# Two-layer graph kernel: column halves stored in another order by block, and second-layer masks read from the ring

## The chip, the cores and the metric

One core of a Trainium2 chip runs the kernel. The metric is the device time of one execution in microseconds. Three runs of the kernel before took 457.03, 455.23 and 456.34 us; their median is 456.34 us.

## The reference, cut to what matters

`x` is 4096 x 64, `adj` is 4096 x 4096 of zeros and ones (symmetric here, with ones on the diagonal, about one entry in 500 set). A first layer is graph attention over a second set of 4096 embeddings, a second layer is a sum over neighbours:

```python
h = jnp.maximum(_layernorm(x), 0.0)
Wh, We = h @ W, entity_embs @ W
scores = (Wh @ a1)[:, None] + (We @ a2)[None, :]
e = jnp.where(scores > 0, scores, ALPHA * scores)
e = jnp.where(adj > 0, e, NEG_BIG)
x = x + elu(softmax(e, axis=1) @ entity_embs + h)
h = jnp.maximum(_layernorm(x), 0.0)
x = x + (adj == 1) @ h + h
```

The second layer needs `h` of a row only after the first layer is done for that row, and all of `adj` a second time.

## The kernel before

**First layer.** The 4096 rows are taken in five blocks of 512, 512, 1024, 1024 and 1024 rows (`HALVES`), the 4096 columns in 32 tiles of 128. The loop runs over 160 steps n, 32 for each block: block 0 has steps 0 to 31, block 2 steps 64 to 95, block 3 steps 96 to 127, block 4 steps 128 to 159. In a step VectorE makes y from a tile of the masks and the scores (L788), ScalarE takes its exponential (L570), and TensorE multiplies it with the embeddings and adds to the block's accumulators (L1042). `yp` has four buffers (`YS`), so VectorE can be four steps ahead of TensorE. Each engine has one program, written out in order by the same loop; a step's extra work is placed by tables of step numbers.

**Masks.** `adj` lies in HBM transposed, as 64 chunks of 128 x 2048 int32 (1 MB each), which a GpSimd-issued DMA turns into bf16 in one of 23 buffers of `am`, the ring (`load`, L344 to 351). A buffer is free when y of its last step has been made. Blocks 2 to 4 have 16 chunks each, one for two steps. Before VectorE makes y it puts the row's shift into the chunk by an exclusive or over all of it (`put_shift`, L698 to 704), so from then on the chunk holds no plain zeros and ones. The shift of a block is found ahead of it: TensorE sums all its masks by column group (`biggest`, L897), VectorE reads the sums (`read_sums`, L667), TensorE turns them (`turn`, L909), VectorE takes the largest (`largest`) and works out the shift (`shifts`), TensorE spreads it to rows (`v_rows`, L917), ScalarE copies it to `vx` (L497), and VectorE does the lone rows (L714) and the first `put_shift`. For block 3 the last sums are at step 88 and `v_rows` at 94, for block 4 at 120 and 126.

**Between blocks.** After a block, ScalarE copies its row sums and numerators out (`sums_out`, L508 and L511) behind the exponential of the next block's second step, and TensorE's second pair of matmuls of the new block waits for that, since it writes into a bank just read. Then the block's rows go through inverse, elu, layer norm and a split into three bf16 parts `h3` (L720 to L758, by the steps in `FIN`): `h` of block 2 is complete at step 110, of block 3 at step 142, of block 4 in the tail.

**Second layer.** It is cut into 32 pieces (p, j): output rows of pair p (1024 rows), neighbours of column half j (512 columns). A piece can run once `h` of half j is there. It is four calls of `neighbours` (L950 to L972), each with six matmuls: three parts of `h` times two row halves, the masks as the moving operand. `ORDER` gives the sequence of the pieces and `PIECE_AT` the step at which each of the first 18 begins; each call stands behind the step's L1042 matmuls. The other 14 pieces follow after step 159. The masks of a piece are loaded a second time, as fp8, by GpSimd's queue (`load_edges`, L353 to 367): the first 16 into the four buffers of `edge`, the last 16 into ring buffers no longer needed. To pieces that hold a part of the diagonal GpSimd adds ones (`own`, L435 to L442). `VISITS` names the pieces after which the sum so far is copied out of bank 3 by ScalarE (`move_out`, L543, five steps after the piece begins) and added to `xs` by VectorE (`add_part`, at `PART_AT`).

The lines around the change, as the program has them before:

Of the kernel before, what the change touches and what calls it, by code (L numbers as in the profile page):

```python
# [5 lines left out]
P = 128  # L6
# [15 lines left out]
HALF = 512  # L22
# [19 lines left out]


ORDER = ((0, 0), (0, 1), (1, 0), (1, 1), (2, 0), (2, 1), (3, 0), (3, 1),
# [3 lines left out]
PIECE_AT = (78, 82, 87, 91, 96, 100, 105, 109, 114, 118, 123, 127, 131, 135, 140, 144, 149, 154)  # L48
PIECES = len(PIECE_AT)
VISITS = (1, 3, 5, 7)  # L50
OPENS = (0, 2, 4, 6, 8, 10, 12, 14)
PART_AT = (116, 120, 150)
EDGES = 4
RINGED = 16


def graph_layers(nc, adj_t, xt, ent, w_t, a_cols, eye, out, N, M, D):
# [12 lines left out]
    def width(b):  # L70
        return HALVES[b] * HALF

# [43 lines left out]
    with ctx:  # L116
        def sb(name, shape, dt):
            return ctx.enter_context(nc.sbuf_tensor(name, shape, dt))
# [9 lines left out]
        part = sb("part", [P, NP, HALF], F32)  # L128
# [65 lines left out]


        def ring_chunk(v):
            return NC - RING + v - RINGED

        def edges(v):
            if v < RINGED:  # L200
                flat = edge[:, v % EDGES]
            else:
                flat = am[:, ring_chunk(v) % RING].bitcast(FP8)
            return flat.rearrange("p (t i) -> p t i", t=4)

# [24 lines left out]
        edges_in = [sem(f"edges_in{v}") for v in range(len(ORDER))]  # L230
# [103 lines left out]
        def _(pool):  # L334
# [18 lines left out]
            def load_edges(v):  # L353
                p, j = ORDER[v]
                if v >= RINGED:
                    pool.wait_ge(y_made, step_past(ring_chunk(v)))
                elif v >= EDGES:
                    pool.wait_ge(piece_done, v - EDGES + 1)
# [5 lines left out]
                else:  # L364
                    q = chunk0[p + 1] + 2 * j
# [79 lines left out]
            def edges_at(v):  # L445
                if v >= RINGED:
                    return max(116 + 3 * (v - RINGED), step_past(ring_chunk(v)))
                return PIECE_AT[v - EDGES] + 5 if v >= EDGES else PIECE_AT[v] - 16

            q, v = 16, 0  # L450
            for n in range(STEPS_ALL):
# [4 lines left out]
                while v < len(ORDER) and edges_at(v) <= n:  # L456
                    load_edges(v)
                    v += 1
# [5 lines left out]
            for w in range(v, len(ORDER)):  # L464
                load_edges(w)
# [7 lines left out]
        def _(act):  # L473
# [92 lines left out]
            for n in range(STEPS_ALL):  # L566
# [3 lines left out]
                sc.activation(y, y, ACT.Exp, bias=tbias[:, jt:jt + 1]).then_inc(exp_done, 1)  # L570
# [34 lines left out]
        def _(dve):  # L605
# [171 lines left out]
            for n in range(STEPS_ALL):  # L777
# [10 lines left out]
                v.scalar_tensor_tensor(out=yp[:, n % YS, 0:W], in0=s8b[:, b % 2, 0:W], scalar=t8neg[:, jt:jt + 1],  # L788
# [38 lines left out]
            link(add_part(len(PART_AT)))  # L827
# [7 lines left out]
        def _(pe):  # L835
# [49 lines left out]
            def biggest(b, k):  # L885
# [7 lines left out]
                for i in range(m):  # L893
                    for g in range(4):
                        jt = 4 * k + g
                        at = jt % T * W + i * HALF
                        mm = t.matmul(pa[g * KC:(g + 1) * KC, i], gtab[:, jt],  # L897
# [52 lines left out]
            def neighbours(v, i):  # L950
                p, j = ORDER[v]
                jt = j * SUB + i
                if i == 0:
                    pe.wait_ge(edges_in[v], 32 if p == 0 else 16)
# [7 lines left out]
                    if v == 10:  # L962
                        pe.wait_ge(gmax_ready, NB)
                    if v == 14:
                        pe.wait_ge(num_sb, first[NB - 2] + 2)
                for k in range(3):
                    for s in range(2):
                        mm = t.matmul(gather(v)[s * D:(s + 1) * D, :], h3[:, jt, k * D:(k + 1) * D],  # L968
                                      edges(v)[:, i, s * HALF:(s + 1) * HALF],
# [45 lines left out]
            for n in range(STEPS_ALL):  # L1015
# [22 lines left out]
                for h in range(first[b], first[b + 1]):  # L1038
# [3 lines left out]
                    mm = t.matmul(acc(h)[0:D + 1, :], enta[:, jt], yp[:, n % YS, i * HALF:(i + 1) * HALF],  # L1042
# [65 lines left out]
```

## Time and profile before

| | |
|---|---|
| Median of three runs | 456.34 us |
| The profiled execution | 455.4 us |
| its span in the trace | 453.6 us |
| TensorE matmul busy | 414.5 us |
| VectorE busy | 317.7 us |
| ScalarE busy | 196.0 us |
| GpSimd busy | 126.9 us |
| Read from HBM | 136.63 MB |
| Mean granted TensorE clock | 0.969 |

The span is what the trace covers, from the first to the last instruction; the profiled execution's own time is 1.8 us more. A row of the timeline merges neighbouring instructions of one line: its start, its length, and in brackets how long the engine had been idle before it and who ended that. A matmul of 32-bit numbers is two instructions, so a step of a 1024-row block is four L1042 rows (x4). In the stretches, PEclk is the granted clock as a share of 2.4 GHz.

### The profile page before, as it was taken

The page shows a single profiled execution, that of the slowest core. Times are in us where ns is not written, and L with a number is a line of the kernel's source. Part 1 is how long each engine was busy: PE and PEld are TensorE (multiplying, and loading weights), DVE is VectorE, ACT ScalarE, POOL GpSimd, SP SyncE. Part 2 cuts the span into 40 slices and gives each one's busy share as a digit, 9 for nine tenths or more (in the row PEclk, how much of TensorE's full clock was granted, in tenths as well). Part 3 has the DMA queues.
Part 4 walks back from the last instruction along what each step waited for, and adds up shares of the span by engine and source line. Part 5 has one row for each costly group of instructions (what it writes and reads, how often), then busy time and mean ns, then how long its engine had stood idle before and what let it go on. Part 6 is the DMA issues. An engine that isn't in the chain of part 4 may idle for free. (4 is left out here: it accounts for less than half of the span.)

```text
span 453.6 us, 4680 instructions
## 1 busy us (share of the span) xinstructions
PE 414.5 (91%) x1786; PEld 143.1 (32%) x1791; DVE 317.7 (70%) x379; ACT 196.0 (43%) x250; POOL 126.9 (28%) x190
## 2 busy tenths in 40 slices
PE   2895997989878899999799999999699999999997
PEld 1562522223212232223122322232123222224564
DVE  3555779998899989659759576767958778723211
ACT  1310454665555656424644644424544544433200
POOL 7599200103022186111102320122042662000400
PEclk9879699999999999999989999999899999999999
DMA  8999999646459999799968998354539999999111
GB/s 270 214 212 215 214 214 171 107 84 102 81 92 149 154 142 161 100 144 159 137 108 85 117 148 124 40 49 45 46 30 103 108 107 106 105 107 108 18 44 50
DMA packets 25382, 54.09 MB, mean 119 GB/s; under 512 B 1872, under 2 KB 10128, under 8 KB 25104
## 3 DMA queue, kind: packets, MB, share of 16 engines
q0 software_dynamic: 24192, 50.34, 79.2%
q1 hardware_dynamic: 1008, 3.42, 2.0%
q8 instruction: 14, 0.23, 0.2%
q10 hardware_dynamic: 160, 0.03, 0.0%
q14 instruction: 8, 0.07, 0.0%
HBM read 136.63 MB, written 1.05 MB: 304 GB/s over the span
## 5 line engine op out<-in xcount | busy, mean ns | idle before, releaser
L1042 PE MATMUL pb<-yp,enta 128*65 128x512 f32 x512 | 247.4, 609 | 18.0 <-ACT yp L570 11.7
L570 ACT ACTIVATE yp<-yp,tbias 128x1024 f32<-128x1024 f32 (+1 forms) x160 | 153.9, 979 | 126.8 <-DVE yp L788 125.8
L788 DVE SCALAR_TENSOR_TENSOR yp<-s8b,t8neg,am 128x1024 f32<-128x1024 f32 (+1 forms) x160 | 168.4, 1079 | 31.4 <-PE pb L1042 29.4
L1042 PEld LDWEIGHTS pb<-yp,enta 128*65 128x65 f32 x512 | 61.9, 138 | 154.3 <-issue 104.3
L703 DVE TENSOR_TENSOR am<-am,vx 128x2048 uint16<-128x2048 uint16 x64 | 79.0, 1234 | 0.7 <-ACT vx L497 0.7
L351 POOL DMA_DIRECT2D am<-adj_t x64 | 35.4, 557 | 130.3 <-DVE yp L788 130.3
L968 PE MATMUL pb<-edge,h 128*64 128x512 fp8e4 x288 | 40.9, 392 | 0.0
L366 POOL DMA_DIRECT2D edge<-adj_t x12 | 8.7, 725 | 79.2 <-PE pb L968 54.1
L968 PEld LDWEIGHTS pb<-edge,h 128*64 128x64 bf16 x288 | 12.3, 109 | 44.4 <-issue 39.6
L968 PE MATMUL pb<-am,h 128*64 128x512 fp8e4 x192 | 22.7, 381 | 0.0
L968 PE MATMUL pa<-am,h 128*64 128x512 fp8e4 x192 | 21.7, 380 | 0.0
L897 PE MATMUL pa<-am,gtab 128*32 128x512 bf16 x256 | 20.7, 392 | 0.0
L431 POOL TENSOR_SCALAR rstd<-rstd 128x8 f32<-128x8 f32 x5 | 2.1, 418 | 58.1 <-ACT rstd L529 58.0
L968 PEld LDWEIGHTS pb<-am,h 128*64 128x64 bf16 x192 | 11.4, 110 | 13.6 <-issue 6.8
L968 PEld LDWEIGHTS pa<-am,h 128*64 128x64 bf16 x192 | 11.8, 110 | 10.2 <-issue 2.5
L442 POOL TENSOR_TENSOR edge<-edge,eyeb 128x128 fp8e4<-128x128 fp8e4 x16 | 15.0, 964 | 0.1
L667 DVE TENSOR_SCALAR gmax<-pa,wk 128x1024 f32<-128x1024 int32 (+1 forms) x5 | 5.4, 1071 | 13.2 <-PE pa L897 13.2
L968 PE MATMUL pa<-edge,h 128*64 128x512 fp8e4 x96 | 14.1, 402 | 0.0
L745 DVE TENSOR_TENSOR rs<-pa,rstd 128x512 f32<-128x512 f32 (+1 forms) x5 | 2.9, 585 | 15.2 <-POOL rstd L432 15.2
L729 DVE TENSOR_TENSOR ta<-num,pa 128x512 f32<-128x512 f32 x5 | 3.4, 686 | 12.1 <-PE pa L933 12.1
L897 PEld LDWEIGHTS pa<-am,gtab 128*32 128x32 bf16 x256 | 4.2, 94 | 23.9 <-issue 23.8
L489 ACT COPY s8b<-pa 128x512 f32<-128x512 f32 x8 | 4.7, 583 | 16.1 <-PE pa L875 16.1
(144 smaller groups left out, 292.2 us busy)
## 6 DMA issues: line engine op xcount, KB each, us to landing
am<-adj_t POOLq DMA_DIRECT2D x76, 512.0 KB, 9.8
edge<-adj_t POOLq DMA_DIRECT2D x12, 512.0 KB, 8.1
edge<-adj_t POOLq DMA_DIRECT2D x8, 256.0 KB, 7.6
am<-adj_t POOLq DMA_DIRECT2D x8, 256.0 KB, 23.9
enta<-ent SPq DMA_DIRECT2D x1, 1040.0 KB, 5.1
xs<-xt SPq DMA_DIRECT2D x1, 1024.0 KB, 8.3
out<-yp SPq DMA_DIRECT2D x4, 256.0 KB, 2.0
mats<-eye SPq DMA_DIRECT2D x1, 256.0 KB, 5.4
```

What stands on the lines that cost most here:

```text
L351: pool.dma_start(am[:, q % RING], adj_t[q]).then_inc(landed[q % RING], 16)
L366: pool.dma_start(edges(v).rearrange("p (c t) i -> p c (t i)", c=2), adj_t[q:q + 2].rearrange("c p n -> p c n")).then_inc(edges_in[v], 16)
L442: g.tensor_tensor(e, e, eyeb[:], ALU.add, saturate=False).then_inc(own_ready, 1)
L489: sc.copy(s8b[:, b % 2, i * HALF:(i + 1) * HALF], bank_s(b, i)).then_inc(s8_ready, 1)
L570: sc.activation(y, y, ACT.Exp, bias=tbias[:, jt:jt + 1]).then_inc(exp_done, 1)
L667: link(v.tensor_scalar(gmax[:, 0:W], sums, wk[:], None, ALU.min))
L703: v.tensor_tensor(at, at, vx[:, b % 2, 0:width(b)].bitcast(U16).unsqueeze(1).to_broadcast([P, tiles(b), width(b)]), ALU.bitwise_xor).then_ ...
L729: link(v.tensor_tensor(ta[:], num[:], turned, ALU.mult))
L788: v.scalar_tensor_tensor(out=yp[:, n % YS, 0:W], in0=s8b[:, b % 2, 0:W], scalar=t8neg[:, jt:jt + 1], in1=am[:, (chunk0[b] + c) % RING, jt ...
L897: mm = t.matmul(pa[g * KC:(g + 1) * KC, i], gtab[:, jt], am[:, (chunk0[b] + jt // T) % RING, at:at + HALF], start=(k == 0), stop=(k == NQ ...
L968: mm = t.matmul(gather(v)[s * D:(s + 1) * D, :], h3[:, jt, k * D:(k + 1) * D], edges(v)[:, i, s * HALF:(s + 1) * HALF], start=(v in OPENS ...
L1042: mm = t.matmul(acc(h)[0:D + 1, :], enta[:, jt], yp[:, n % YS, i * HALF:(i + 1) * HALF], start=(jt == 0), stop=(jt == NT - 1))
```

## The change

The chunks of blocks 2 to 4 hold their column halves in another order (`COLUMNS`): block 2 ends with halves 0 and 1, block 3 with 0 to 3, block 4 has 6, 7 and then 0 to 5. Everything that goes by column tile (`t8neg`, `tbias`, `gtab`, `enta`) is indexed through `tile_at`. So chunks whose halves have their `h` early now lie in the ring, loaded and not yet shifted, when their piece can run. 12 pieces (`DIRECT`) read their masks there, as bf16, and are not loaded a second time; `put_shift` of each of their chunks waits for the piece. The order of the pieces, the steps at which they begin, the steps of the loads and the banks of the sums are changed to fit: three partial sums are moved out instead of four, and pair 3 keeps its bank.

```diff
+COLUMNS = ((0, 1, 2, 3, 4, 5, 6, 7), (0, 1, 2, 3, 4, 5, 6, 7), (2, 3, 4, 5, 6, 7, 0, 1),
+           (4, 5, 6, 7, 0, 1, 2, 3), (6, 7, 0, 1, 2, 3, 4, 5))
...
-ORDER = ((0, 0), (0, 1), (1, 0), (1, 1), (2, 0), (2, 1), (3, 0), (3, 1),
...
+ORDER = ((1, 0), (1, 1), (0, 0), (0, 1), (2, 0), (2, 1), (2, 2), (2, 3), (3, 0), (3, 1), (3, 2), (3, 3),
+         (0, 2), (0, 3), (3, 4), (3, 5), (1, 2), (1, 3),
...
-PIECE_AT = (78, 82, 87, 91, 96, 100, 105, 109, 114, 118, 123, 127, 131, 135, 140, 144, 149, 154)
+PIECE_AT = (70, 80, 85, 89, 96, 100, 111, 115, 120, 124, 128, 132, 136, 140, 144, 148, 152, 156)
-VISITS = (1, 3, 5, 7)
-OPENS = (0, 2, 4, 6, 8, 10, 12, 14)
-PART_AT = (116, 120, 150)
+DIRECT = (0, 1, 4, 5, 6, 7, 8, 9, 10, 11, 14, 15)
+LOADED = tuple(v for v in range(len(ORDER)) if v not in DIRECT)
+VISITS = (1, 3, 7)
+OPENS = (0, 2, 4, 8, 12, 16, 22)
+PART_AT = (118, 122, 154)
-RINGED = 16
+RINGED = 6
+LOAD_AT = (48, 54, 62, 70, 94, 98)
...
+        def masks(v, i, s):
+            if v in DIRECT:
+                at = i % 2 * 2 * HALF + s * HALF
+                return am[:, chunks_of(*ORDER[v])[i // 2] % RING, at:at + HALF]
+            return edges(v)[:, i, s * HALF:(s + 1) * HALF]
...
-            return pb[:, 3] if v <= VISITS[-1] else (pb[:, 3], pa[:, 0], pa[:, 1], pb[:, 2])[p]
+            return pb[:, 3] if v <= VISITS[-1] else (pa[:, 0], pa[:, 1], pb[:, 2], pb[:, 3])[p]
...
             def put_shift(b, c):
                 q = chunk0[b] + c
                 if c == 0:
                     dve.wait_ge(vx_ready, first[b + 1])
+                for w in DIRECT:
+                    if q in chunks_of(*ORDER[w]):
+                        dve.wait_ge(piece_done, w + 1)
...
-            link(add_part(len(PART_AT)))
...
                 if i == 0:
-                    pe.wait_ge(edges_in[v], 32 if p == 0 else 16)
+                    if v in DIRECT:
+                        for q in chunks_of(p, j):
+                            pe.wait_ge(landed[q % RING], 16 * (q // RING + 1))
+                    else:
+                        pe.wait_ge(edges_in[v], 32 if p == 0 else 16)
```

Where the instructions stand is shown at three places. In the changed program the lines are numbered anew: L897 is L927, L917 is L947, L968 (the six matmuls of a `neighbours` call) is L1002, L1042 is L1076, L543 is L569, L570 is L597, L497 is L523, L508 and L511 are L534 and L537.

TensorE, from the mask sums of step 92 over `v_rows` (step 94) to the first matmuls of step 96, before:

```order
L897 MATMUL pa<-am,gtab 32x512 x8
L1042 MATMUL pb<-yp,enta 65x512 x2
L968 MATMUL pb<-edge,h 64x512 x6
L1042 MATMUL pb<-yp,enta 65x512 x2
L968 MATMUL pb<-edge,h 64x512 x6
L917 MATMUL pa<-vd,onesb 128x512 x2
L1042 MATMUL pb<-yp,enta 65x512 x2
L968 MATMUL pb<-edge,h 64x512 x6
L1042 MATMUL pb<-yp,enta 65x512 x2
L897 MATMUL pa<-am,gtab 32x512 x8
L1042 MATMUL pb<-yp,enta 65x512 x2
```

and now:

```order
L927 MATMUL pa<-am,gtab 32x512 x8
L1076 MATMUL pb<-yp,enta 65x512 x2
L1002 MATMUL pb<-edge,h 64x512 x6
L1076 MATMUL pb<-yp,enta 65x512 x2
L947 MATMUL pa<-vd,onesb 128x512 x2
L1076 MATMUL pb<-yp,enta 65x512 x4
L927 MATMUL pa<-am,gtab 32x512 x8
L1076 MATMUL pb<-yp,enta 65x512 x2
```

The calls of `neighbours` behind steps 93 and 94 are gone from here. Block 2 has 16 of them before and now: before at steps 78 to 85 and 87 to 94, now at 70 to 73, 80 to 83 and 85 to 92.

ScalarE, the exponentials and copies from step 80 to 97 (vx is the shift, part the partial sum, rows and num the old block's sums), before:

```order
L570 ACTIVATE yp<-yp,tbias 128x1024 x7
L543 COPY part<-pb 128x512
L570 ACTIVATE yp<-yp,tbias 128x1024 x8
L497 CAST vx<-pa 128x512 x2
L570 ACTIVATE yp<-yp,tbias 128x1024
L543 COPY part<-pb 128x512
L570 ACTIVATE yp<-yp,tbias 128x1024
L508 COPY rows<-pb 1x512 x2
L511 COPY num<-pb 64x512 x2
```

and now:

```order
L597 ACTIVATE yp<-yp,tbias 128x1024 x5
L569 COPY part<-pb 128x512
L597 ACTIVATE yp<-yp,tbias 128x1024 x9
L569 COPY part<-pb 128x512
L597 ACTIVATE yp<-yp,tbias 128x1024
L523 CAST vx<-pa 128x512 x2
L597 ACTIVATE yp<-yp,tbias 128x1024 x2
L534 COPY rows<-pb 1x512 x2
L537 COPY num<-pb 64x512 x2
```

The second copy of a partial sum has moved from behind the exponential of step 96 to behind that of step 94, ahead of the two copies to vx.

TensorE, from step 104 on, before:

```order
L897 MATMUL pa<-am,gtab 32x512 x8
L943 MATMUL pa<-mats,tm 128x2 x4
L946 MATMUL pa<-mats,ta 128x128 x4
L1042 MATMUL pb<-yp,enta 65x512 x4
L968 MATMUL pb<-edge,h 64x512 x6
L1042 MATMUL pb<-yp,enta 65x512 x2
L968 MATMUL pb<-edge,h 64x512 x6
L1042 MATMUL pb<-yp,enta 65x512 x2
L968 MATMUL pb<-edge,h 64x512 x6
L897 MATMUL pa<-am,gtab 32x512 x8
L1042 MATMUL pb<-yp,enta 65x512 x2
```

and now:

```order
L927 MATMUL pa<-am,gtab 32x512 x8
L973 MATMUL pa<-mats,tm 128x2 x4
L976 MATMUL pa<-mats,ta 128x128 x4
L1076 MATMUL pb<-yp,enta 65x512 x8
L927 MATMUL pa<-am,gtab 32x512 x8
L1076 MATMUL pb<-yp,enta 65x512 x2
L905 MATMUL pa<-h,w 128x512
L1076 MATMUL pb<-yp,enta 65x512 x4
L905 MATMUL pa<-h,w 128x512
L1076 MATMUL pb<-yp,enta 65x512 x2
L1002 MATMUL pb<-am,h 64x512 x6
```

Steps 105 to 110 have lost their `neighbours` calls (step 104 had none before either); the next one stands behind step 111.

## Rows read from the trace of the kernel before

**Rows 1.** Page of the profile: part 1, and what HBM moved

```profile
PE 414.5 (91%) x1786; PEld 143.1 (32%) x1791; DVE 317.7 (70%) x379; ACT 196.0 (43%) x250; POOL 126.9 (28%) x190
...
HBM read 136.63 MB, written 1.05 MB: 304 GB/s over the span
```

**Rows 2.** Waits: engine line waited for: us in total, times, longest us

```profile
DVE yp L788 <- PE pb L1042: 29.4, 28, 2.0
...
PE pb L1042 <- ACT num L511: 6.1, 2, 3.1
```

**Rows 3.** Stretches: length, busy us per engine, PEclk, DMA share, GB/s

```profile
160.00:180.00 20.00, 20.00 (x71) 6.08 (x72) 18.36 (x18) 12.30 (x15) 16.01 (x15) 1.00 1.01 162
...
220.00:240.00 20.00, 16.74 (x65) 4.25 (x68) 14.74 (x16) 9.68 (x12) 1.78 (x3) 0.91 0.71 102
```

**Rows 4.** TensorE timeline, steps 69 and 78: start, us, what, [idle before <- whom]

```profile
151.60 3.65 PE L1042 MATMUL pb<-yp,enta 128*65 128x512 f32 x8 [1.20 <-ACT yp L570]
...
174.42 0.84 PE L968 MATMUL pb<-edge,h 128*64 128x512 fp8e4 x6
```

**Rows 5.** TensorE timeline, steps 85 to 87, one slice and none

```profile
193.11 1.93 PE L1042 MATMUL pb<-yp,enta 128*65 128x512 f32 x4
194.98 0.84 PE L968 MATMUL pb<-edge,h 128*64 128x512 fp8e4 x6
195.74 3.65 PE L1042 MATMUL pb<-yp,enta 128*65 128x512 f32 x8
199.32 0.84 PE L968 MATMUL pb<-edge,h 128*64 128x512 fp8e4 x6
```

**Rows 6.** TensorE timeline, steps 88 to 96, the first border

```profile
200.09 0.61 PE L897 MATMUL pa<-am,gtab 128*32 128x512 bf16 x8
...
218.07 0.38 PE L917 MATMUL pa<-vd,onesb 128*128 128x512 bf16 x1 [0.16 <-issue]
...
223.54 1.07 PE L1042 MATMUL pb<-yp,enta 128*65 128x512 f32 x2 [0.20 <-ACT yp L570]
227.67 1.97 PE L1042 MATMUL pb<-yp,enta 128*65 128x512 f32 x2 [3.06 <-ACT num L511]
```

**Rows 7.** ScalarE timeline at the same border

```profile
215.38 2.35 ACT L570 ACTIVATE yp<-yp,tbias 128x1024 f32<-128x1024 f32 x2 [2.65 <-DVE yp L788]
218.27 1.07 ACT L497 CAST vx<-pa 128x512 bf16<-128x512 f32 x2 [0.54 <-remote]
...
225.84 1.18 ACT L508 COPY rows<-pb 1x512 f32<-1x512 f32 x2
```

**Rows 8.** VectorE timeline at the same border

```profile
200.76 1.28 DVE L667 TENSOR_SCALAR gmax<-pa,wk 128x1024 f32<-128x1024 int32 x1 [4.39 <-PE pa L897]
...
219.38 0.42 DVE L714 TENSOR_SCALAR rows<-vx 3x1024 bf16<-3x1024 bf16 x1 [2.83 <-ACT vx L497]
```

**Rows 9.** TensorE timeline, steps 120 to 128, the second border

```profile
298.30 0.61 PE L897 MATMUL pa<-am,gtab 128*32 128x512 bf16 x8
...
314.82 0.38 PE L917 MATMUL pa<-vd,onesb 128*128 128x512 bf16 x1 [0.16 <-issue]
...
321.46 1.07 PE L1042 MATMUL pb<-yp,enta 128*65 128x512 f32 x2 [0.97 <-ACT yp L570]
325.60 1.18 PE L1042 MATMUL pb<-yp,enta 128*65 128x512 f32 x2 [3.06 <-ACT num L511]
```

**Rows 10.** ScalarE timeline at the second border

```profile
316.21 1.05 ACT L497 CAST vx<-pa 128x512 bf16<-128x512 f32 x2
```

**Rows 11.** VectorE timeline, y of step 108

```profile
257.57 1.28 DVE L788 SCALAR_TENSOR_TENSOR yp<-s8b,t8neg,am 128x1024 f32<-128x1024 f32 x1
```

**Rows 12.** TensorE timeline, step 108

```profile
264.45 1.93 PE L1042 MATMUL pb<-yp,enta 128*65 128x512 f32 x4
```

**Rows 13.** GpSimd timeline, own() of the first piece

```profile
165.26 4.16 POOL L442 TENSOR_TENSOR edge<-edge,eyeb 128x128 fp8e4<-128x128 fp8e4 x4
```

**Rows 14.** VectorE timeline beside it

```profile
164.37 1.53 DVE L788 SCALAR_TENSOR_TENSOR yp<-s8b,t8neg,am 128x1024 f32<-128x1024 f32 x1
```

More of the change, by code:

```diff
@@ L71, in width, with tile_at, place @@
         return HALVES[b] * HALF
+    def tile_at(b, jt):
+        return COLUMNS[b][jt // SUB] * SUB + jt % SUB
+    def place(b, j):
+        return COLUMNS[b].index(j)
     def tiles(b):
@@ L127, in graph_layers @@
         edge = sb("edge", [P, EDGES, 2 * CHUNK], FP8)
-        part = sb("part", [P, NP, HALF], F32)
+        part = sb("part", [P, len(VISITS), HALF], F32)
         yp = sb("yp", [P, YS, 2 * HALF], F32)
@@ L192, in graph_layers, with chunks_of, ring_chunk @@
         arep = am[0:D, 22].bitcast(F32)[:, 0:P]
-        def ring_chunk(v):
-            return NC - RING + v - RINGED
+        def chunks_of(p, j):
+            q = chunk0[p + 1] + 2 * place(p + 1, j)
+            return q, q + 1
+        def ring_chunk(u):
+            return NC - RING + u - RINGED
         def edges(v):
-            if v < RINGED:
-                flat = edge[:, v % EDGES]
+            u = LOADED.index(v)
+            if u < RINGED:
+                flat = edge[:, u % EDGES]
             else:
-                flat = am[:, ring_chunk(v) % RING].bitcast(FP8)
+                flat = am[:, ring_chunk(u) % RING].bitcast(FP8)
             return flat.rearrange("p (t i) -> p t i", t=4)
+        def masks(v, i, s):
[3 more added lines that the diff above has]
+            return edges(v)[:, i, s * HALF:(s + 1) * HALF]
         pa = ps("pa", [P, 4, HALF])
@@ L229, in graph_layers @@
         landed = [sem(f"landed{k}") for k in range(RING)]
-        edges_in = [sem(f"edges_in{v}") for v in range(len(ORDER))]
+        edges_in = {v: sem(f"edges_in{v}") for v in LOADED}
         out_done = sem("out_done")
@@ L351, in load, with load_edges @@
                 pool.dma_start(am[:, q % RING], adj_t[q]).then_inc(landed[q % RING], 16)
-            def load_edges(v):
+            def load_edges(u):
+                v = LOADED[u]
                 p, j = ORDER[v]
[L355 to L358, printed above, removed]
+                if u >= RINGED:
+                    pool.wait_ge(y_made, step_past(ring_chunk(u)))
+                elif u >= EDGES:
+                    pool.wait_ge(piece_done, LOADED[u - EDGES] + 1)
                 if p == 0:
@@ L455, in _ @@
                     q += 1
-                while v < len(ORDER) and edges_at(v) <= n:
-                    load_edges(v)
-                    v += 1
+                while u < len(LOADED) and edges_at(u) <= n:
+                    load_edges(u)
+                    u += 1
                 if b >= 1 and jt == FIN[b - 1]["vs"] + 1:
@@ L1076 @@
     r = 0
-    for m in HALVES:
+    for m, order in zip(HALVES, COLUMNS):
         t = 4 // m
-        a = np.asarray(adj)[r:r + m * HALF].reshape(m * HALF, NT // t, t, P).transpose(1, 3, 2, 0)
+        a = np.asarray(adj)[r:r + m * HALF].reshape(m * HALF, M // HALF, HALF)[:, list(order)]
+        a = a.reshape(m * HALF, NT // t, t, P).transpose(1, 3, 2, 0)
         parts.append(a.reshape(NT // t, P, CHUNK))
```

28 lines of the change are left out of this document (13 added, 15 removed), and 3 rows, old and new, of the table ORDER.

## The prediction

> **What bounds the kernel now.** I read part 1 of the page first: TensorE is busy 414.5 of 453.6 us, VectorE 317.7 [rows 1]. Then the stretches: from 160 to 180 us TensorE is busy 20.00 of 20 [rows 3], and the stretches behind it look the same except around two places. Then the waits: VectorE waits for TensorE 28 times [rows 2], so it runs ahead by the four buffers of yp and is held back by TensorE. The TensorE timeline says where that begins: its last plain idle time before a piece is 1.20 us ahead of step 69 [rows 4], and from there to the tail it stands still only at the borders of the last blocks. So from step 70 the time is TensorE's work plus the idle time at the borders. I write "slice" for the six matmuls of `neighbours()` in one step, and "pv" for the step's main matmuls.
>
> A step with a slice takes 195.74 - 193.11 = 2.63 us, two without take 199.32 - 195.74 = 3.58, or 1.79 each [rows 5]. A slice is worth **0.84 us**, wherever it stands.
>
> The two idle places are steps 96 and 128. The first matmul pair of the block waits 0.20 or 0.97 us for the exponential, the second 3.06 us for ScalarE to copy the old accumulator out [rows 6, 9]; both together are the two waits of 6.1 us [rows 2]. What ends there is a chain which starts at the last mask sums (L897, steps 88 and 120): VectorE's read of the sums at 200.76 [rows 8], the turn, the largest, the shift, `v_rows` on TensorE (218.07), the copies to vx on ScalarE (218.27) [rows 7], the lone rows (219.38) [rows 8], two y, and ScalarE's row copies from 225.84 [rows 7]. The pair of matmuls after the wait takes 1.97 us against 1.07 for the pair ahead of it [rows 6], with the granted clock at a mean of 0.91 in that stretch [rows 3].
>
> **The change, part by part.**
>
> *Slices moved.* The table still holds 72 slices in the loop and 56 behind it, so TensorE's sum is unchanged: 0. Four of them now stand at steps 70 to 73. TensorE had no idle time there to be filled (it lies ahead of step 69, [rows 4]), so they gain nothing.
>
> *First border.* Up to step 87 nine slices ran before, eleven will: the last mask sums come 2 x 0.84 = 1.7 us later. From there to the end of the wait the chain is 227.67 - 200.09 = 27.6 us [rows 6]. Inside it TensorE had seven slices to do, now five. The chain passes `v_rows` in TensorE's order, which is now one slice earlier, and ScalarE had waited 0.54 us for it [rows 7]. But the copy of a finished piece (L543), which stood behind the exponential of step 96, is moved between those of 94 and 95, just ahead of the vx copies, and takes about half the 1.18 us of two row copies [rows 7]. It uses up the 0.54. So the chain stays at 27.6 us with two slices less inside: **+1.7 us** of idle time (0.20 and 3.06 become about 2 and 3.1).
>
> *Steps 104 to 110* hold no slice now. VectorE finishes y of step 108 at 257.57 + 1.28 = 258.9, its exponential (half of the 2.35 us of two, [rows 7]) ends at 260.0, and TensorE comes to it at 264.45 [rows 11, 12]: 4.4 us of lead. The slices of 105 to 107 go, 2.5 us; 1.9 are left. After that both engines run at nearly one pace. I take 0.
>
> *Second border.* The chain from the mask sums at 298.30 to 325.60 takes 27.3 us [rows 9]. `v_rows` at 314.82 could be 0.84 later without delaying the vx copies of 316.21 [rows 9, 10], so the chain holds its length. Inside it are now eight slices instead of seven (step 122 was empty), and the eighth fits into the 0.97 us: **-0.8 us**.
>
> *Masks read from the ring as bf16.* No row shows such a slice. The nearest is L897, which streams bf16 columns of the same tile: eight matmuls in two packs of four last 0.61 us [rows 6], 0.305 a pack, against 0.84 / 3 = 0.28 a pair in a slice [rows 5]. The 12 pieces have 12 x 4 x 3 = 144 pairs, so between 0 and 144 x 0.025 = 3.6 us; a pack holds twice the matmuls of a pair, and I take 0.
>
> *Waits.* Each of the 12 pieces waits for two chunks instead of one load. The first slice of a piece, with its waits, starts in the row of 199.32 right when the pv ends [rows 5]: 0. VectorE's `put_shift` waits for the piece at steps 118, 122, 150 and 154. At 118 it already needs the pv of step 114 and now its slice too, 0.84 later. At 150 it needs the slice of 147 instead of the pv of 146: 0.84 + 1.79 + 0.84 = 3.5 us, and TensorE then has three steps of 2.63 in hand, 7.9 us, against some 1.3 us each for the shift, y and the exponential. Hidden. If TensorE's lead work were gone, each hold would cost its 3.5 us.
>
> *Loads and GpSimd.* 12 issues on its queue go. The others are issued behind the chunk loads of their step. No TensorE wait for a chunk is in the rows of the waits after the start: 0. The `own()` additions, 4.16 us a piece, ran beside a y that took 1.53 instead of 1.28 us [rows 13, 14, 11]; they move to steps 83 and 87, where VectorE waits anyway. Two such stretches of some 5 us, a fifth longer, are at most 2 us of VectorE time. TensorE was not idle there, so 0. The Trainium skill, "SBUF — State Buffer", section "Who interferes with whom", says that VectorE and GpSimd share a port pair which one of them takes whole; by that the 2 us are real, and the sum would be 2 us better only if VectorE set the pace at steps 76 to 83.
>
> *One partial sum less*: a copy of 0.6 us and an addition, the last of them behind `lasts`, while TensorE works: 0.
>
> Sum: 1.7 - 0.8 = **+0.9 us**. The profiled execution took 455.4 us, the median of the three runs is 456.34, 0.9 above it. So 456.3 in the first measure and **457.2** as a median.
>
> **Rivals.**
>
> *The empty steps starve TensorE (slower, 0.16).* It decides if y of step 108 comes more than 1.9 us later, relative to TensorE, than in the rows above. The chain of the standard deviation goes over ScalarE and GpSimd just there, and the first border starts it from a longer wait. For it: 1.9 us is the smallest lead of the loop. Against it: nothing in that chain is lengthened. The price is up to the three slices that no longer cover it, 2.5 us: 459.7.
>
> *The slow clock lasts longer behind the first border (slower, 0.05).* The pair there lost 0.9 us [rows 6]; a longer idle stretch ahead of it may cost as much again, and half of that in the next slice: 457.2 + 1.4 = 458.6.
>
> *The first border costs nothing (0.13).* If ScalarE finishes the extra copy while it waits anyway and VectorE was the longer branch, only the second border's gain is left or both cancel: 455.5 to 456.3.
>
> *Transfers were the bound after all (faster, 0.08).* The queues are full from 160 to 180 us (share 1.01, [rows 3]), and 12 loads of 2.1 MB, 25 of the 136.6 MB read [rows 1], go away. If one border wait hung on a late chunk, it would go with its slow pair: -3.06 - 0.9 = -4.0, 452.3. Against it: TensorE is busy 20.00 of 20 in that same stretch. The Trainium skill, the same page, section "A bandwidth-pool intuition that's wrong (but worth ruling out)", calls HBM almost always the end-to-end bottleneck; this trace does not agree after the start, where 304 GB/s [rows 1] go beside a full TensorE.
>
> *The change doesn't do what it says (0.02).* The loads could be issued all the same; the order of GpSimd's queue shows 20 pieces loaded, not 32, so hardly.
>
> **How the numbers follow.** The forecast has 0.56. About 0.5%, 2.3 us, is what a measurement of this kernel can tell from no change. Faster by more: the transfers, 0.08, and 0.02 of scatter (the three runs lie 1.8 us apart). Slower by more needs above 458.6: most of the empty steps (0.14), half of the clock (0.03) and 0.03 for the bf16 bound: 0.20. The rest, 0.70, is the same. The range goes from 0.9 us of scatter below the case 455.5, 454.6, to the bounds of the empty steps and of bf16 (457.2 + 2.5 = 459.7 and 457.2 + 3.6 = 460.8), so 460.8.
>
> **What would show it.** HBM read near 111 MB. L897 of step 88 near 201.8 us. Ahead of the first pair of step 96 about 2 us of idle time, ahead of the second about 3.1, with `v_rows` near 218.9. At step 128 next to nothing ahead of the first pair. No idle time from step 104 to 111. Slices from am that last 0.84 us like those from edge. Wrong would be: an idle TensorE anywhere between steps 70 and 95, or 104 and 120; a slice from the ring clearly above 0.84 us; VectorE waiting at L733 long enough to empty yp; or borders without idle time.

## The result, and the profile after

The changed kernel takes 457.92 us in the median of 8 runs (457.18 to 458.98), the kernel before 455.69 us in 8 runs (455.09 to 457.03), the three of the first section among them. The medians are 2.2 us apart; the ratio on record is 1.0039, 95% interval 1.0024 to 1.0053, which makes it 1.8 us slower. Both are under the 0.5% (2.3 us) that I had put as the bound. The forecast was 457.2 us, 0.9 us slower. Of the difference 0.3 us lies outside the span: the profiled execution took 457.4 us with a span of 455.3, 2.1 us apart where the kernel before had 1.8.

The page of the changed kernel, parts 1, 3 and 5:

```profile
PE 415.3 (91%) x1791; PEld 141.8 (31%) x1791; DVE 316.4 (69%) x378; ACT 194.8 (43%) x249; POOL 115.8 (25%) x178
...
HBM read 111.46 MB, written 1.05 MB: 247 GB/s over the span
...
L733 DVE TENSOR_TENSOR am<-am,vx 128x2048 uint16<-128x2048 uint16 x64 | 78.9, 1233 | 4.8 <-PE pb L1002 4.1
...
L1002 PE MATMUL pb<-am,h 128*64 128x512 bf16 (+1 forms) x432 | 57.2, 390 | 0.0
...
L1002 PE MATMUL pa<-edge,h 128*64 128x512 fp8e4 x96 | 13.4, 387 | 0.0
```

TensorE is as busy as before (415.3 to 414.5 us, [rows 1]); 25.2 MB less are read. A matmul on bf16 masks from the ring lasts 390 ns (the group holds the fp8 ones of bank pb too), one on fp8 masks from `edge` 387. VectorE stood still twice ahead of a `put_shift` (L733), 4.1 us in all.

The TensorE timeline of the changed kernel around the first border; it answers to [rows 4, 6] (L927 is L897, L947 is L917, L1076 is L1042, L1002 is L968):

```profile
151.40 3.65 PE L1076 MATMUL pb<-yp,enta 128*65 128x512 f32 x8 [1.20 <-ACT yp L597]
...
201.72 0.61 PE L927 MATMUL pa<-am,gtab 128*32 128x512 bf16 x8
...
218.61 0.59 PE L947 MATMUL pa<-vd,onesb 128*128 128x512 bf16 x2
...
224.83 1.07 PE L1076 MATMUL pb<-yp,enta 128*65 128x512 f32 x2 [1.65 <-ACT yp L597]
228.96 1.97 PE L1076 MATMUL pb<-yp,enta 128*65 128x512 f32 x2 [3.06 <-ACT num L537]
230.86 1.30 PE L1002 MATMUL pb<-am,h 128*64 128x512 bf16 x6
232.09 1.93 PE L1076 MATMUL pb<-yp,enta 128*65 128x512 f32 x4
```

Step 69 begins at 151.40 instead of 151.60, so 0.2 us are to be added in a comparison. The last mask sums are at 201.72 against 200.09: counted from step 69 1.8 us later, two slices and 0.15 us. The wait ends at 228.96, 27.24 us after them, where it was 27.58. Ahead of the first pair TensorE now stands still for 1.65 us. The second border, answering to [rows 9]:

```profile
294.53 0.61 PE L927 MATMUL pa<-am,gtab 128*32 128x512 bf16 x8
...
317.94 1.07 PE L1076 MATMUL pb<-yp,enta 128*65 128x512 f32 x2 [0.49 <-ACT yp L597]
322.08 1.97 PE L1076 MATMUL pb<-yp,enta 128*65 128x512 f32 x2 [3.06 <-ACT num L537]
323.98 1.49 PE L1002 MATMUL pb<-am,h 128*64 128x512 bf16 x6
325.40 2.91 PE L1076 MATMUL pb<-yp,enta 128*65 128x512 f32 x4
328.24 0.84 PE L1002 MATMUL pb<-am,h 128*64 128x512 bf16 x6
```

Two rows of the kernel before that the comparison below needs, the main matmuls of step 97 and the slice of step 129:

```profile
230.96 1.93 PE L1042 MATMUL pb<-yp,enta 128*65 128x512 f32 x4
...
330.83 0.84 PE L968 MATMUL pa<-edge,h 128*64 128x512 fp8e4 x6
```

At the second border the chain takes 322.08 - 294.53 = 27.55 us against 27.30, the first pair waits 0.49 us against 0.97, and the pair behind the wait takes 1.97 us where it took 1.18. Steps 104 to 111 and step 108, answering to [rows 11, 12]:

```profile
255.48 7.03 PE L1076 MATMUL pb<-yp,enta 128*65 128x512 f32 x16
...
262.99 1.93 PE L1076 MATMUL pb<-yp,enta 128*65 128x512 f32 x4
```

Four steps without a slice follow each other in 7.03 us, and no idle time stands ahead of any of these rows. The two spans differ by 1.7 us. Cut at the rows shown, they add up as follows:

| stretch of TensorE's timeline | before, us | now, us | difference, us |
|---|---|---|---|
| start to step 69 | 151.60 | 151.40 | -0.20 |
| step 69 to the end of the first wait | 76.07 | 77.56 | +1.49 |
| from there to the main matmuls of step 97 | 3.29 | 3.13 | -0.16 |
| from there to the end of the second wait | 94.64 | 89.99 | -4.65, with five slices fewer (4.20): -0.45 |
| from there to the slice of step 129 | 5.23 | 6.16 | +0.93 |
| from there to the end of the span | 122.77 | 127.06 | +4.29, with five slices more (4.20): +0.09 |

So the first border costs 1.49 us: the sums 1.83 later, less 0.34 for a shorter chain. The second gives back 0.45: the idle time ahead of its first pair falls from 0.97 to 0.49. Together that is 1.04 us. The slow rows behind the two waits give -0.16 and +0.93, start and end -0.20 and +0.09.

### The profile page after: what moved, and what is told of

Same layout as the page of the kernel before. It is cut to its first block and busy times, and to the rows that moved or that the text cites. A ratio compares the mean times of both kernels' runs of the same rounds, so it can differ in the third digit from the quotient of the medians.

```text
span 455.3 us, 4672 instructions
## 1 busy us (share of the span) xinstructions
PE 415.3 (91%) x1791; PEld 141.8 (31%) x1791; DVE 316.4 (69%) x378; ACT 194.8 (43%) x249; POOL 115.8 (25%) x178
## 5 line engine op out<-in xcount | busy, mean ns | idle before, releaser
L1076 PE MATMUL pb<-yp,enta 128*65 128x512 f32 x512 | 250.0, 613 | 18.9 <-ACT yp L597 12.7
L597 ACT ACTIVATE yp<-yp,tbias 128x1024 f32<-128x1024 f32 (+1 forms) x160 | 153.5, 977 | 129.1 <-DVE yp L819 128.0
L1076 PEld LDWEIGHTS pb<-yp,enta 128*65 128x65 f32 x512 | 61.9, 138 | 154.3 <-issue 106.5
L733 DVE TENSOR_TENSOR am<-am,vx 128x2048 uint16<-128x2048 uint16 x64 | 78.9, 1233 | 4.8 <-PE pb L1002 4.1
L380 POOL DMA_DIRECT2D am<-adj_t x64 | 35.4, 559 | 172.8 <-DVE yp L819 172.8
L1002 PE MATMUL pb<-am,h 128*64 128x512 bf16 (+1 forms) x432 | 57.2, 390 | 0.0
L1002 PEld LDWEIGHTS pb<-am,h 128*64 128x64 bf16 x432 | 21.9, 110 | 50.6 <-issue 39.8
L1002 PE MATMUL pa<-am,h 128*64 128x512 fp8e4 x192 | 21.6, 380 | 0.0
L927 PE MATMUL pa<-am,gtab 128*32 128x512 bf16 x256 | 20.9, 395 | 0.0
L396 POOL DMA_DIRECT2D am<-adj_t x10 | 7.1, 713 | 49.1 <-DVE yp L819 43.4
L472 POOL TENSOR_TENSOR edge<-edge,eyeb 128x128 fp8e4<-128x128 fp8e4 x16 | 16.0, 1026 | 0.1
L1002 PEld LDWEIGHTS pa<-am,h 128*64 128x64 bf16 x192 | 11.8, 110 | 9.8 <-issue 2.0
L1002 PE MATMUL pa<-edge,h 128*64 128x512 fp8e4 x96 | 13.4, 387 | 0.0
L927 PEld LDWEIGHTS pa<-am,gtab 128*32 128x32 bf16 x256 | 4.2, 94 | 25.5 <-issue 25.4
L542 ACT ACTIVATE tm<-ta 128x512 f32<-128x512 f32 x5 | 3.1, 628 | 19.6 <-DVE ta L760 19.6
L750 DVE STREAM_TRANSPOSE gmax<-rows 64x512 f32<-64x512 f32 x5 | 3.5, 708 | 10.7 <-ACT rows L534 10.4
```

The costliest lines, as they stand in the source:

```text
L380: pool.dma_start(am[:, q % RING], adj_t[q]).then_inc(landed[q % RING], 16)
L396: pool.dma_start(edges(v).rearrange("p (c t) i -> p c (t i)", c=2), adj_t[q:q + 2].rearrange("c p n -> p c n")).then_inc(edges_in[v], 16)
L472: g.tensor_tensor(e, e, eyeb[:], ALU.add, saturate=False).then_inc(own_ready, 1)
L597: sc.activation(y, y, ACT.Exp, bias=tbias[:, at:at + 1]).then_inc(exp_done, 1)
L733: v.tensor_tensor(at, at, vx[:, b % 2, 0:width(b)].bitcast(U16).unsqueeze(1).to_broadcast([P, tiles(b), width(b)]), ALU.bitwise_xor).then_ ...
L750: link(v.transpose(turn32, inv))
```

## Experiments

Twelve experiments on three chips, all against the kernel before on the same chip.

**Is it the slices inside the first chain?** Two kernels move pieces 1 to 3. In e1 seven slices stand between the sums of step 88 and the border, as before the change:

```diff
-PIECE_AT = (70, 80, 85, 89, 96, ...)
+PIECE_AT = (70, 82, 87, 91, 96, ...)
```

In e5 there are three:

```diff
-PIECE_AT = (70, 80, 85, 89, 96, ...)
+PIECE_AT = (70, 79, 83, 87, 96, ...)
```

> The changed kernel with pieces 1 to 3 begun at steps 82, 87 and 91 as before instead of 80, 85 and 89, so that seven slices stand again between the last mask sums of step 88 and the border of step 96, and the copy of the partial sum is behind step 96 again. My theory (the slices missing inside that fixed chain cost 0.84 us each): the idle time ahead of the first pair of step 96 falls from 1.65 to near 0.2 us and the whole is 1.3 us faster than the changed kernel, span near 454.0, ratio to the kernel before about 1.001. Rival (the changed kernel's loss sits elsewhere, in the slow clock or in the reads from the ring): span stays at 455.3.

> The same place the other way: pieces 1 to 3 begin at steps 79, 83 and 87, so that only three slices stand between the mask sums of step 88 and the border. My theory: two slices more are taken out of the chain's shadow, 2 x 0.84 = 1.7 us more idle time ahead of the first pair of step 96 (near 3.3 us), span near 456.9. Rival (the border's idle time does not depend on the slices): 455.3 as in the changed kernel.

Measured: e1 456.21 us (12 runs), ratio 0.9992 (0.9979 to 1.0006); e5 459.38 us (6 runs), ratio 1.0063 (1.0043 to 1.0083); between them, on the same chip, the changed kernel with added loads (e4, below) 457.64. That kernel has 0.3 us less outside its span than the other two, so the spans are compared, in runs of the same mean clock, 0.966: 454.25 us for e1 (8 runs), 455.70 for e4 (10 runs, and 455.70 for the changed kernel itself in 7), 457.16 for e5 (5 runs). So 1.45 us back and 1.46 more, for two slices each way. The idle rows of e5 at the border:

```profile
221.30 3.65 PE L1076 MATMUL pb<-yp,enta 128*65 128x512 f32 x8 [0.69 <-ACT yp L597]
...
227.59 1.07 PE L1076 MATMUL pb<-yp,enta 128*65 128x512 f32 x2 [2.10 <-ACT yp L597]
231.73 1.97 PE L1076 MATMUL pb<-yp,enta 128*65 128x512 f32 x2 [3.06 <-ACT num L537]
```

0.69 + 2.10 us of idle time stand ahead of the first pair instead of 1.65, and the 3.06 of the second pair is unchanged. From step 69 (152.81 us here) the second pair's wait ends after 78.92 us instead of 77.56, 1.36 more and not the 1.7 expected: the copy of the partial sum has left the chain in e5, which is 0.32 us shorter for it (26.92). In e1 the first pair waits 0.20 us, as before the change:

```profile
224.03 1.07 PE L1076 MATMUL pb<-yp,enta 128*65 128x512 f32 x2 [0.20 <-ACT yp L597]
228.16 1.07 PE L1076 MATMUL pb<-yp,enta 128*65 128x512 f32 x2 [3.06 <-ACT num L537]
```

The slices inside the chain are shown to be the cause at this border, at 0.73 us each by the runs. e1's chain is again 27.58 us long. e1 is level with the kernel before.

**The second chain.** The additions of partial sums are taken out of it:

```diff
-PART_AT = (118, 122, 154)
+PART_AT = (114, 118, 154)
```

> The changed kernel with the two first additions of partial sums on VectorE at steps 114 and 118 instead of 118 and 122, so that none lies inside the chain from the mask sums of step 120 to the border of step 128. My theory: the addition of 0.68 us at 299.99 us lengthened that chain; without it the second pair of step 128 starts 0.6 us earlier, idle ahead of the first pair falls from 0.49 to near 0, span near 454.7. Rival (VectorE has slack there, as I had costed it): no change, 455.3.

Measured: 457.46 us (12 runs), ratio 1.0022 (1.0007 to 1.0037), 0.2 us below the kernel with added loads on the same chip. By spans at the mean clock 0.966 it is 455.34 us (10 runs) against 455.70 (10 runs): 0.4 us of the 0.5 that the chain became shorter, and hardly clear of the scatter (454.5 to 456.4 in e2's ten runs). The profiled execution is the slowest of the twelve (458.51 us). In it the chain is shorter, and the time is lost again behind the borders:

```profile
295.80 0.61 PE L927 MATMUL pa<-am,gtab 128*32 128x512 bf16 x8
...
318.70 1.07 PE L1076 MATMUL pb<-yp,enta 128*65 128x512 f32 x2
322.84 1.97 PE L1076 MATMUL pb<-yp,enta 128*65 128x512 f32 x2 [3.07 <-ACT num L537]
324.74 1.49 PE L1002 MATMUL pb<-am,h 128*64 128x512 bf16 x6
326.16 3.25 PE L1076 MATMUL pb<-yp,enta 128*65 128x512 f32 x4
```

From the sums to the second pair 27.04 us instead of 27.55, and no idle time ahead of the first pair. But the matmuls of step 129 take 3.25 us instead of 2.91, and the rows behind the first border 0.17 us more than in the changed kernel: more of the work ran at the low clock. From step 69 to the end this execution takes 456.4 - 152.5 = 303.9 us, like the changed kernel's. That the shorter chain is lost on average is not shown: between the theory (0.6) and the rival (0), the runs lean to the theory.

**Transfers.** 12 loads come back, to a buffer of their own, at steps 66 to 123:

```diff
+            def load_again(k):
+                q = 36 + 2 * k
+                if k >= 1:
+                    pool.wait_ge(dup_in, 16 * k)
+                pool.dma_start(dup[:].rearrange("p (c n) -> p c n", c=2),
+                               adj_t[q:q + 2].rearrange("c p n -> p c n")).then_inc(dup_in, 16)
```

> The changed kernel with 12 loads of 2 MB read from HBM added on the same queue, to a buffer that nobody reads, at steps 66 to 123, so that about as much is read as before. My theory (transfers set the pace nowhere after the start): no change beyond 0.3 us, 455.3, with HBM read back near 136.6 MB. Rival (fewer transfers give time back which something else eats): 2 us or more slower than the changed kernel, 457.3 and up, with waits of TensorE or VectorE for a landed chunk.

Measured: 457.64 us (12 runs), ratio 1.0028 (1.0013 to 1.0043); its profiled span is that of the changed kernel, 455.3 us, and so is the median of its spans, 455.8. Outside the span it has 1.8 us again, like the kernel before, where the changed kernel has 2.1: those 0.3 us come and go with the twelve loads. How is not shown.

```profile
HBM read 136.63 MB, written 1.05 MB: 302 GB/s over the span
```

The 25.2 MB are back and cost nothing in the span. From step 66 on, transfers set the pace nowhere; the start was not tested.

**The clock behind the borders.** 12 matmuls which compute nothing stand where TensorE waits 3.06 us, in the changed kernel (e7, again as e11), in the kernel before (e9) and in e1 (e10):

```diff
+                    if jt == 0 and h >= 3 and i == 1:
+                        pe.wait_ge(vx_ready, first[b + 1])
+                        for k in range(KEEP):
+                            t.matmul(bank_s(b, k % 2), onesb[:], vd[:, 0:SUB].rearrange("p c k -> p (c k)"),
+                                     start=True, stop=True)
                     if jt == 0 and h >= 3:
                         pe.wait_ge(num_sb, h - 2)
```

> The changed kernel with 12 matmuls of 128x512 bf16 added on TensorE between the first and the second pair of steps 96 and 128, into a bank that nobody reads. They take no time from anything else (3.06 us of waiting stand there, they need about 2.7 us) and compute nothing. My theory: the granted clock then stays up behind both borders, the pairs and slices there take 1.07 and 0.84 us instead of 1.97 and 1.30 to 1.49, which gives back about 1.5 us at the first border and 2.6 at the second, 4 us in all, span near 451.3; the waits for ScalarE end where they ended. Rival (the slow rows behind the border are not the clock but the restart of the pipe): no change, 455.3.

Measured: 454.97 us (5 runs), ratio 0.9955 (0.9942 to 0.9968). Useless work makes the changed kernel 3 us faster. Two stretches of 12 us, one over each border, in the table of stretches of the changed kernel (columns as in [rows 3]):

```profile
224.00:236.00 12.00, 8.11 (x23) 2.04 (x24) 9.54 (x10) 7.68 (x9) 1.79 (x3) 0.86 0.85 119
318.00:330.00 12.00, 8.94 (x23) 2.21 (x24) 8.65 (x9) 6.90 (x8) 2.17 (x3) 0.72 1.06 85
```

The same stretches of e7:

```profile
224.00:236.00 12.00, 9.88 (x44) 3.13 (x44) 11.00 (x11) 8.05 (x9) 1.79 (x3) 1.00 0.83 123
318.00:330.00 12.00, 11.47 (x44) 3.55 (x44) 8.77 (x9) 6.91 (x9) 2.17 (x3) 1.00 1.04 85
```

And e7's TensorE timeline at the second border:

```profile
318.97 2.75 PE L1078 MATMUL pa<-vd,onesb 128*128 128x512 bf16 x12
322.19 1.07 PE L1081 MATMUL pb<-yp,enta 128*65 128x512 f32 x2 [0.47 <-ACT num L538]
323.20 0.84 PE L1003 MATMUL pb<-am,h 128*64 128x512 bf16 x6
```

The granted clock is 1.00 (2.4 GHz) where it had a mean of 0.86 and 0.72, that is, part of the stretch at 1.2 GHz. The pair behind the wait takes 1.07 us, not 1.97, and still begins at 322.19: the wait for ScalarE ends as before. So behind both borders the slow rows are the clock. In the changed kernel it fell while TensorE stood still: taken microsecond by microsecond at the second border, the granted clock is 1.00 up to 320, 0.79 to 321, 0.50 up to 327, 0.79 to 328 and 1.00 again, with the wait over at 322.08. In the kernel before it fell at the second border only after TensorE had begun again, between 326 and 327 us with the wait over at 325.60, and was back between 329 and 330; so its pair there took 1.18 us and only the slice and the matmuls behind it were slow.

I expected 4 us. From step 69, where the start is left out, to the end of the span it is 452.9 - 152.9 = 300.0 us instead of 455.3 - 151.4 = 303.9, the 3.9 us expected; the start took 1.5 us of them back in this execution. Over all runs the gain in the span is 3.0 us (a mean of 452.9 in e7 and in e11, 455.9 and 456.0 in the two batches of the changed kernel). The length of the start varies from 151.0 to 152.9 us in the profiles of the changed kernel and its variants, though none of their edits but e4's first load stands in it; why is open.

> The kernel before with the 12 idle matmuls in both waits, so that no border lowers the clock. My theory: the runs of the kernel before lie between 455.3 and 457.8 us by how much of the work behind the borders meets the low clock (their mean clock goes from 0.969 to 0.962), and with the clock held the borders' idle time alone is left: 0.75 us less than the changed kernel with the same matmuls, so span near 452.0 and a time near 453.9, and less scatter. Rival (the changed kernel's loss is a matter of the clock only): the same 452.9 and 455.0 as the changed kernel with them.

> The changed kernel with the 12 idle matmuls once more, beside the kernel before with them on the same chip. Theory: 455.0 us again, 0.8 to 1.1 us above the kernel before with them (0.75 for the borders, up to 0.3 outside the span). Rival (clock only): no difference between the two.

> The changed kernel with the idle matmuls and with seven slices inside the first chain. Theory: the first border's 1.3 us come back, free of the clock: 1.3 us below the changed kernel with the idle matmuls, near 453.7, and 0.3 to 0.6 below the kernel before with them in span, since the second border has its eighth slice. Rival: part of the 2.1 us between the changed kernel and the one with seven slices was the clock, and here it is under 0.8.

Measured on one chip: e9 454.21 us (9 runs, ratio 0.9946, 0.9927 to 0.9965), e11 454.89 us (12 runs, 0.9963, 0.9947 to 0.9978), e10 453.49 us (6 runs, 0.9938, 0.9916 to 0.9960). From step 69 to the end of the span, where the start is left out, e9 takes 452.1 - 153.2 = 298.9 us, e11 452.9 - 152.9 = 300.0 and e10 451.0 - 152.5 = 298.5. With the clock held, the change costs 1.1 us of span, and giving the first chain its seven slices takes 1.5 us off. Both are what the rows say: 1.49 - 0.45 + 0.09 = 1.13 by the table above, and 1.48 from step 69 to the end of the first wait (77.56 us in e11, 76.08 in e9 and e10). The 0.75 and 1.3 of the theories left out the 0.15 us ahead of the first chain and took 0.59 for the second border. The mean clock is 0.977 in all runs of e11, but 0.973 to 0.977 in e9 and e10, though in their profiles it is 1.00 over both borders: the clock of an execution varies in other places too. In the start of these profiles, between 20 and 60 us, it lies between 0.66 and 0.84.

> The changed kernel again, as it is, beside the others and the kernel before on one chip. Theory: its runs scatter with the mean clock as those of the kernel before do, 0.966 to 0.963 with 457.5 to 459, and its distance to the kernel before comes out between 0.7 and 2.5 us by the clocks that the two happen to draw. Rival (the longer low clock at its second border is its own): its mean clock never reaches the 0.969 of the kernel before, on any chip.

Measured: 457.89 us (12 runs), ratio 1.0036 (1.0021 to 1.0052). Its profile has the slow rows the other way round:

```profile
224.00:236.00 12.00, 7.88 (x21) 1.77 (x21) 9.77 (x10) 7.92 (x9) 1.79 (x3) 0.72 0.83 117
318.00:330.00 12.00, 8.45 (x28) 2.05 (x28) 9.93 (x10) 8.05 (x9) 2.17 (x3) 0.86 1.18 94
```

Now the mean is 0.72 over the first border and 0.86 over the second, in the same program. Put in order by the mean clock of the whole execution, the runs give (of the kernel before those beside the experiments, of the changed kernel those of the result and e12):

| mean granted clock | kernel before: runs, mean us | changed kernel: runs, mean us |
|---|---|---|
| 0.969 | 15, 455.3 | none |
| 0.965 | 18, 456.2 | none |
| 0.966 | 15, 457.1 | 16, 457.8 |
| 0.962 or 0.963 | 16, 457.8 | 4, 459.0 |

The kernel before lies anywhere between 455 and 458 us by how much of its work meets the low clock, and the execution profiled of it was one of the luckiest. Over all these runs the mean clock of the two kernels is the same, 0.9654, and their mean spans are 454.8 and 456.0 us: 1.2 apart, near the 1.1 that the borders give without the clock. So the 0.93 us behind the second border is a draw of the two executions that were profiled. What differs is the spread: the changed kernel and its variants with the longer idle time at the first border (e2, e4, e5) never had 0.969 or 0.965 in 50 runs, where 33 of 64 of the kernel before had, and e1, with the old idle time there, had 0.970 in 4 of 12. That speaks for the idle time as what keeps them from those cases; how, no run shows.

**A version that beats both.** If TensorE waits there, the slices that come next can run there. The four of steps 96 to 99 and of 128 to 131 are put between the two pairs, in the changed kernel (e3), in the kernel before (e6, there seven, those of 96 to 99 and of 128 to 130), and with the changes of e1 and e2 on top (e8):

```diff
+FILL = {96: ((4, 0), (4, 1), (4, 2), (4, 3)), 128: ((10, 0), (10, 1), (10, 2), (10, 3))}
+MOVED = sum(FILL.values(), ())
...
+                    if i == 1 and n in FILL:
+                        for k in FILL[n]:
+                            neighbours(*k)
                     if jt == 0 and h >= 3:
                         pe.wait_ge(num_sb, h - 2)
...
-                    if at <= n < at + SUB:
+                    if at <= n < at + SUB and (v, n - at) not in MOVED:
```

> The changed kernel with the four slices of steps 96 to 99 and the four of 128 to 131 placed between the first and the second pair of steps 96 and 128, where TensorE waits 3.06 us. My theory: eight slices leave the rest of the loop, six to eight times 0.77 to 0.84 us are gained, about 6 us, and the clock stays up as with added matmuls, 4 us: span near 446, if VectorE keeps up in steps 97 to 103 and 129 to 135. Rival (VectorE becomes the bound behind the border, since it starts the block late and has the inverses and the weighting there): only the clock's 4 us are gained, near 451.

> The same in the kernel before: the four slices of steps 96 to 99 and those of 128 to 130 stand inside the two waits. My theory: the same gain as in the changed kernel less one slice, so the kernel before with it stays 1 to 2 us ahead of the changed kernel with it, span near 445 to 446. Rival (reading from the ring pays once TensorE is no longer held): the changed kernel with filled waits is the faster.

> The changed kernel with filled waits, the old steps of pieces 1 to 3 (seven slices inside the first chain) and the partial sums added four steps earlier. My theory: another 1.3 us for the first border and 0.5 us for the second on top of the filled waits, near 444.5 and the fastest of all. Rival (with the waits filled the chain on VectorE and ScalarE sets the borders): within 0.5 us of the kernel with filled waits alone.

Measured on one chip: e3 446.85 us (5 runs), ratio 0.9777 (0.9764 to 0.9791); e6 446.89 us (4 runs), 0.9775 (0.9758 to 0.9791); **e8 444.78 us** (4 runs), 0.9735 (0.9717 to 0.9753). e8 around its first border:

```profile
222.93 1.07 PE L1081 MATMUL pb<-yp,enta 128*65 128x512 f32 x2 [0.20 <-ACT yp L599]
223.93 2.78 PE L1004 MATMUL pb<-am,h 128*64 128x512 bf16 x24
227.06 4.51 PE L1081 MATMUL pb<-yp,enta 128*65 128x512 f32 x10 [0.35 <-ACT num L539]
```

24 matmuls stand where nothing stood, 0.35 us of waiting are left, and the four steps' slices are gone from behind the border: five pairs (two and a half steps) follow in 4.51 us, at the full clock. For e3 the sum is 8 slices x 0.84 = 6.7 us and the 3 to 4 us of clock that e7 showed, against 11 measured. The slices alone are seen beside e11, where the clock is held as well: from step 69 to the end e3 takes 444.7 - 151.6 = 293.1 us, 6.9 less than the 300.0. e8 is 2.1 us below e3, 1.8 expected. e3 and e6 are level, though e6 fills one slice less; I had expected e6 to be 1 to 2 us ahead, where the 1.1 us that e11 and e9 differ by, less a slice of 0.84, leave 0.3. e3 gives VectorE no trouble:

```profile
234.74 0.69 DVE L761 TENSOR_TENSOR ta<-num,pa 128x512 f32<-128x512 f32 x1 [0.83 <-PE pa L965]
```

its wait for TensorE at the weighting is 0.83 us, where it was 4.78.

## Why the prediction was right, point by point

**What bounds.** Right. From step 70 the time is TensorE's work and the idle time at the borders; e5, e1 and the filled waits move it as slices do.

**Slices moved to steps 70 to 73: nothing gained.** Right. The sums of step 88 came 1.8 us later, two slices and 0.15 us. The 0.15 is the price of a slice, which isn't 0.84 "wherever it stands": the two of steps 72 and 73 break up a run of main matmuls without slices, and such a run is faster in a row (four steps in 7.03 us) than in twos (3.65). Four steps took 160.42 to 167.38 us before, the same four with the two slices take 161.76 to 170.55 now, 1.83 us more.

**First border, +1.7 us.** Right in mechanism, 0.2 too high: 1.49. The sums came 1.83 us later, not 1.68, and the chain did not hold its 27.6 us but came out at 27.24. The step that was off is "it uses up the 0.54". The copy takes 0.47 us, from 218.06 to 218.53, and a part of that fell into a gap in which ScalarE would have waited for y: the second exponential begins 1.52 us after the first, where it began 1.2 after it before. So the copy delays the chain by 0.32, while the wait for `v_rows` that went was worth 0.64: the copies to vx begin 17.86 us after the sums here, 18.18 in the kernel before, and 17.54 in e5, which has neither. These are the rows:

```profile
217.01 1.15 ACT L597 ACTIVATE yp<-yp,tbias 128x1024 f32<-128x1024 f32 x1 [2.65 <-DVE yp L819]
218.06 0.56 ACT L569 COPY part<-pb 128x512 f32<-128x512 f32 x1
218.53 1.15 ACT L597 ACTIVATE yp<-yp,tbias 128x1024 f32<-128x1024 f32 x1
219.58 1.06 ACT L523 CAST vx<-pa 128x512 bf16<-128x512 f32 x2
```

**Second border, -0.8 us.** Right in sign; -0.45. The chain took 0.25 of the 0.84 us back (0.84 - 0.25 = 0.59), and the six slices fewer between the first border and the sums of step 120 took 4.90 us off and not 5.04. The step that failed is "one partial sum less ... 0": I had costed what goes and not looked where the others land. `PART_AT` moves an addition from step 120 to step 122, into the chain:

```profile
299.99 0.68 DVE L795 TENSOR_TENSOR xs<-xs,part 128x512 f32<-128x512 f32 x1
300.59 2.47 DVE L819 SCALAR_TENSOR_TENSOR yp<-s8b,t8neg,am 128x1024 f32<-128x1024 f32 x2
302.98 1.21 DVE L733 TENSOR_TENSOR am<-am,vx 128x2048 uint16<-128x2048 uint16 x1
```

It puts 0.60 us between a `put_shift` and y. The chain grew by 0.25 only, because `own()` had run beside it before and no longer does. The rows of the kernel before:

```profile
305.24 3.51 POOL L442 TENSOR_TENSOR edge<-edge,eyeb 128x128 fp8e4<-128x128 fp8e4 x4
...
303.75 2.63 DVE L788 SCALAR_TENSOR_TENSOR yp<-s8b,t8neg,am 128x1024 f32<-128x1024 f32 x2
306.31 1.43 DVE L703 TENSOR_TENSOR am<-am,vx 128x2048 uint16<-128x2048 uint16 x1
```

where the changed kernel has 2.47 and 1.21. The Trainium skill, "SBUF — State Buffer", "Who interferes with whom", says that a VectorE instruction with two inputs in SBUF contends with a GpSimd instruction that reads SBUF. The rows agree, and give the size, which the section does not give for this case: 0.16 and 0.22 us beside four additions of 3.51 us together. No run takes `own()` out alone, so this part is read from rows and not tested. So the port's price was real and inside a chain, where I had looked for it at steps 76 to 83 alone.

**Steps 104 to 110: 0.** Right. y of step 108 is finished at 259.4, its exponential at 260.6, TensorE comes at 262.99: 2.4 us of lead, 1.9 forecast. The first rival did not come true.

**bf16 masks: 0 (of 0 to 3.6).** Right. A slice takes 0.84 us from either place.

**Waits at `put_shift`: hidden.** Right. VectorE stands still at steps 150 and 154 for 2.05 us each, forecast as a hold of 3.5 us less the y in it, and TensorE has no idle time behind them.

**The clock.** Wrong by a size. I had given a longer low clock 0.05 and a price of 1.4 us, at the first border, as if its length followed from the idle time. It came at the second, for 0.93 us, in the profiled execution, and at the first in another execution of the same program, where the longer low clock hit the second border less. What failed is taking one profiled execution of the kernel before as its state: it had 0.969, which 15 of 64 runs have. Over all runs the clock gave neither kernel an advantage.

**Transfers.** The rival is refuted by e4. The sentence of the Trainium skill on HBM ("SBUF — State Buffer", "A bandwidth-pool intuition that's wrong (but worth ruling out)") does not hold for this kernel behind step 66: 25.2 MB more or less leave its span at 455.3 us. The 304 GB/s that I set against it are the mean over the whole span, start included.

**The sum.** 0.9 forecast for the borders; 1.04 by the rows, 1.1 with the clock held. The two errors, 0.2 too much at the first border and 0.4 too much gain at the second, partly cancel. Another 0.3 us is outside the span, a term that the forecast did not have; that gives some 1.4 of the 1.8 to 2.2 us measured, and the rest is within their scatter. That the forecast time, 457.2, lies 0.7 below the measured 457.92 and not further is in part luck: it started from 456.34, and the median of the kernel before came down to 455.69.

## What to carry to other kernels

Where a chain over several engines has a fixed length, count the independent work of the bound engine that is issued inside it: each piece moved out is paid nearly in full (1.45 us for two slices of 0.84), and each moved into the wait is free until the wait is used up. Before moving an operation on an engine that "has slack", look whether its new place is in such a chain. And a wait of a few us on TensorE is to be filled rather than shortened: here filling two waits of 3 us gave 10 to 12 us, since it also kept the clock up.

## What the runs showed of the hardware that was not expected

Work that nobody needs made both kernels faster, the kernel before by 2.5 us (e9, by its ratio of 0.9946) and the changed one by 3.0 (e11 against e12 on one chip, 454.89 and 457.89), because the granted clock stayed at 2.4 GHz behind the borders. Without it the clock fell in some executions while TensorE stood still and in others only after it had begun again, at waits of the same 3.06 us; when it falls late, the rows behind it are slow all the same. An unchanged program spreads over 455 to 458 us with its mean clock, of which the borders are a part only: with them held at 1.00 the runs of e9 still spread over 1.8 us. And the time outside the span was 1.8 us for the kernel before, its variants and e4 (in three of e9's nine runs 2.0 to 2.7), but 2.1 us for the changed kernel and its other variants; e4 shows that it goes with the twelve loads, and why is open.
